# A batch loop written out in full on all five engines of a gated cross-attention kernel

## What is computed

```python
x = x + tanh(g_xattn[0]) * L0_xattn(layernorm(x), ctx)   # 4 heads of 64, q/k/v/o projections
x = x + tanh(g_ffn[0])   * L0_ffn(layernorm(x))          # x @ (W + low-rank product) + b
x = x + tanh(g_xattn[1]) * L1_xattn(layernorm(x), ctx)   # one head, softmax over 375 keys
x = x + tanh(g_ffn[1])   * L1_ffn(layernorm(x))          # 16-head self-attention + top 2 of 8 experts
```

## Time and profile before

| what | value |
|---|---|
| runs shown | 920.01, 922.46, 924.37 us; median 922.46 |
| profiled execution: its own time | 923.47 us |
| profiled execution: span, first to last instruction | 921.5 us |
| mean granted TensorE clock | 0.977 |
| busy over the span: PE, DVE, ACT, POOL | 846.2 (92%), 785.2 (85%), 563.2 (61%), 392.7 (43%) us |
| instructions recorded | 34388 |
| DMA packets: the kernel's own (q1), instruction fetch (q8, q14) | 41256; 18 and 11 |

### The profile page before, as it was taken

How to read it: one execution, slowest core, us unless ns; L and a number is a source line. 1 busy time by engine, 2 the same in 40 slices (tenths; PEclk the granted TensorE clock), 3 DMA queues, 4 the chain that set the end, 5 groups by cost and what they waited for, 6 DMA issues and landing times. The chain is left out here.

```text
span 921.5 us, 34388 instructions
## 1 busy us (share of the span) xinstructions
PE 846.2 (92%) x11764; PEld 666.0 (72%) x11764; DVE 785.2 (85%) x1910; ACT 563.2 (61%) x1230; POOL 392.7 (43%) x603
## 2 busy tenths in 40 slices
PE   4678999999999999999999999999999999999876
PEld 2467777778777777787777778777777787777654
DVE  3588989989998989899899998998999889888654
ACT  2444666666666666666666666666666666666443
POOL 3311545433455453344554433445544334454433
PEclk9789999999999999999999999999999999999987
DMA  7311222121112211212222122122221211111100
GB/s 257 114 61 57 66 79 66 59 73 61 58 61 75 75 62 62 68 57 63 64 75 74 52 73 63 53 70 66 75 70 54 75 60 56 61 59 56 39 6 6
DMA packets 41285, 61.82 MB, mean 67 GB/s; under 512 B 6158, under 2 KB 28036, under 8 KB 41128
## 3 DMA queue, kind: packets, MB, share of 16 engines
q1 hardware_dynamic: 41256, 61.43, 20.9%
HBM read 37.77 MB, written 3.67 MB: 45 GB/s over the span
## 5 line engine op out<-in xcount | busy, mean ns | idle before, releaser
L1317 POOL TENSOR_TENSOR acc<-part,acc 112x256 f32<-112x256 f32 x256 | 212.4, 830 | 298.9 <-DVE acc L1163 275.3
L820 ACT ACTIVATE part<-bankE,cgS 112x256 f32<-112x256 f32 x256 | 107.2, 473 | 3.0 <-PE bankE L329 2.3
L1266 POOL TENSOR_SCALAR ln_ve<-ln_mv 112x1 f32<-112x1 f32 x128 | 33.9, 265 | 174.5 <-DVE ln_mv L967 173.2
L329 PE MATMUL bankE<-wexs_hi,xT_hi 128*112 128x512 f16 x256 | 99.3, 388 | 3.4 <-ACT part L820 3.4
L1270 POOL TENSOR_TENSOR ln_rs<-ln_ve,cst 112x1 f32<-112x1 f32 x128 | 94.5, 738 | 10.7
L329 PE MATMUL bankE<-wexs_hi,xT_lo 128*112 128x512 f16 x256 | 97.7, 382 | 0.0
L329 PE MATMUL bankE<-wexs_lo,xT_hi 128*112 128x512 f16 x256 | 97.7, 382 | 0.0
L1067 DVE TENSOR_TENSOR p_lo<-p2T,p_hi 112x896 f16<-112x896 f32 x64 | 67.6, 1094 | 9.6 <-ACT p_hi L811 9.6
L1130 DVE TENSOR_REDUCE mx<-quad 112x8 f32<-112x896 f32 x64 | 69.6, 1088 | 1.0
L740 ACT ACTIVATE p0T<-quad 125x896 f32<-125x896 f32 x64 | 46.2, 722 | 38.6 <-PE quad L445 38.6
L973 DVE TENSOR_SCALAR xn<-x,ln_mv,ln_rs 112x256 f32<-112x256 f32 x96 | 54.9, 572 | 5.9 <-POOL ln_rs L1270 2.0
(11 more groups left out here) (239 smaller groups left out, 3275.5 us busy)
## 6 DMA issues: line engine op xcount, KB each, us to landing
ctf<-in_ctx_T SPq DMA_DIRECT2D x32, 375.0 KB, 3.1
ctn<-in_ctx_n SPq DMA_DIRECT2D x32, 375.0 KB
kvB<-kvA SPq DMA_DIRECT2D x32, 281.2 KB, 2.4
kc<-kvB SPq DMA_DIRECT2D x32, 187.5 KB
xin<-in_x SPq DMA_DIRECT2D x32, 112.0 KB, 2.0
x<-in_x SPq DMA_DIRECT2D x32, 112.0 KB, 2.1
out_x<-xout SPq DMA_DIRECT2D x32, 112.0 KB, 1.9
wex<-in_w_exp SPq DMA_DIRECT2D x1, 2048.0 KB, 9.9
```

Source lines behind the costliest of these rows:

```text
L329: last = mm(o, w, m, start=(n == 0), stop=(n == len(terms) - 1))
L820: act.activation(part[:, e, :], bankE[0:LQ, n * D:(n + 1) * D], ACT.Identity, scale=cgS[:, e:e + 1])\
L1317: pool.tensor_tensor(acc[:], part[:, 2 * j + n, :], acc[:], ALU.add).then_inc(moe_sum[j].sem, 1)
```

## The change

The hardware loops go. `iterations` and SP's loop become Python loops over all 36 iterations, so that each engine's program is one straight line, with every batch number an integer: counts in waits and addresses in DMAs become constants, the register steps that worked them out and the branch at the end of each iteration are gone. The order of steps in each iteration, the conditions of the waits and all operations on data are as they were.

```diff
-PEEL = 5
@@
         def iterations(eng, body):
-            for i in range(PEEL):
-                body(*at(i))
-            with eng.Fori(PEEL, NB) as i:
-                body(i, i - 1, i - 2, i - 3, i - 4)
-            for i in range(NB, NB + STAGES - 1):
+            for i in range(NB + STAGES - 1):
                 body(*at(i))
@@
-            for i in range(PEEL):
+            for i in range(NB - 1):
                 body(*at(i), True)
-            with sp.Fori(PEEL, NB - 1) as i:
-                body(i, i - 1, i - 2, i - 3, i - 4, True)
             for i in range(NB - 1, NB + STAGES - 1):
                 body(*at(i), False)
```

## The result

The changed kernel is slower: 950.93 us (median; 944.67 to 954.28) against 921.40 us (920.01 to 924.37) for the kernel before on the same chip, a ratio of 1.031 with a 95% interval of 1.025 to 1.037. The forecast of 935.5 had the sign and the place of the loss, but less than half its size, and the median lies 0.9 us above the range of 919 to 950.

The account below looks back on a forecast made before the run. A closed chain of two DMA copies and nearly full PE work, 26.45 us an iteration, was taken as the bound. 923.5 + 1.6 (steps, waits) + 11.5 (packets) = 936.6, less 1.0 offset: 935.5 us, range 919 to 950.

Parts of the forecast that it names:

- the sign and the place of the loss: Slower by 1.4%, through instruction packets delaying copies in the chain through SP; slower by over 0.5% had chance 0.70.
- The bound: Steady iterations: a closed chain from scores1_T through SP and two DMAs (10.97 us), then PE alone (15.48), sets the 26.45.
- Register steps, branches and waits, +1.6 us: Steady loop: PE part gains 0.14 us, DMA part loses 0.20; +0.06 an iteration over 27, bounds -3.8 to +5.4.
- Packets, count and rhythm: DMA queues in all 27 iterations: near 3 q8 and 2 q14 instruction packets each, drifting slowly, so hits come in phases.
- How often, and what one costs, 0.43 us an iteration: Copy landings: 0.53 q8 hits at 0.65 us plus 0.27 q14 hits at 0.3 an iteration; 11.5 us over 27.
- The clock: PE's wait before max0_T: one hit was not enough to lower PE's clock, so nothing was counted for it.
- the rival at 958 us: Fetch does more than touch landings: sequencers stop for code or two hits lower PE's clock; about 958 us, chance 0.08.
- Packets that miss: q8 packets stay off the copies or delays are absorbed; only small parts, -3.8 to +5.4, remain: about 924 us, chance 0.20.
- Branches on the path: PE's hand-over between iterations: removing 27 branches of 0.215 us saves 5.8 us, giving about 917 us; chance 0.10.

Follow-up runs that it names:

- the loop of three: The looped kernel before, with three iterations instead of one in its loop body on every engine: 983.55 us, ratio 1.064.
- the phase was locked at 1.0 to 1.5: Changed kernel plus 17 waits in each PE iteration from the sixth on and 96 instructions at PE's start: 995.71 us, ratio 1.077 to before.
- the locked clear phase: Changed kernel plus 17 waits in each PE iteration from the sixth on, keeping q8 packets off the copy: 932.64 us, ratio 1.009 to before.

## Why the prediction was right and wrong

*The bound.* Right. The chain of the earlier trace rows is what every loss with one buffer ran through, but for the loop of three; with it cut, PE's wait at `max0_T` was gone and the time fell by 27.6 us against before.

*Register steps, branches and waits, +1.6 us.* Right in size. PE's part is shorter by about 0.14 us a pass without clock falls (447.1 for 449.3 with one fall of 2.5 in it), SP's hops and the unhindered landing longer by 3.3 and 4.2 us over 29 passes, the hop behind it shorter by 1.5; together some +2. A clean pass of the changed kernel takes 26.49 to 26.51 us (the 16th, 18th and 20th) and one of before 26.44 to 26.49, some 0.04 us less, where the forecast had 0.06. The reading of the earlier trace rows was too coarse in one point: the 0.14 us are not PE's own. With PE alone straight its part stays at 15.47 us, and with PE looped and the rest straight it is 15.34.

*Packets, count and rhythm.* Right: near 3 on q8 and 2 on q14 an iteration, in phases. Passes 6 to 15 were hit, 16 to 20 nearly clean, 21 to 29 hit again, the 15 iterations worked out above.

*How often, and what one costs, 0.43 us an iteration.* This step failed first. It treated the packets as spread evenly over the iteration and priced each hit alike, 0.65 us. In the profiled run the 29 passes had 0.59 us of late landing each. A q8 packet started in the 3.5 us behind the issue in 18 of 29 passes, and in none in the 2.1 us before it (0.62, not 0.53), and the price hangs on where in them it starts:

| start of the q8 packet after the issue, us | passes | mean delay of the landing, us |
|---|---|---|
| 0 to 0.5 | 9 | 0.31 |
| 0.5 to 1.0 | 4 | 1.02 |
| 1.0 to 1.5 | 4 | 1.98 |
| later | 1 | 0.26 |

A mean over the 18 gives 0.83 us (in some a q14 packet lay there too). Where the phase was locked at 1.0 to 1.5, 16 passes had 2.05 us on average and 2.65 at most, above the 1.8 of the earlier trace rows that I had taken as the price of a square hit. The place is not the whole of it: one packet of that kernel started 2.10 us after the issue and went with a delay of 2.58. Against 11.5 us forecast, the late landings took 17.1 in 29 passes.

*The clock.* The second failed term, and the larger one for the median: "PE stood 1.96 us at full clock, so one hit is not enough". In the changed kernel the clock fell at 402, 566 and 812 us, each time behind a late landing (waits of 2.92, 1.60 and 2.76 us; one of 3.01 had no fall behind it), and PE's part took 16.47, 17.83 and 16.54 us instead of 15.3: 4.9 us. The other three timed runs had mean clocks about 0.011 below the profiled one; 0.011 of 943 is 10 us at most, and their median, 951.37, is 6.7 us longer. No trace of those runs shows where their clock fell, so that the remaining 6 us are clock is inferred from its mean. So of the two mis-sized terms the late landings took 5.6 us more than forecast, and the clock, put at nothing, 4.9 us in the profiled execution and, by that inference, about 11 in the median. This was the rival at 958 us, to which I gave 0.08; its clock part was real, its stops of sequencers were not, except in the loop of three.

*The rivals.* "Packets that miss" is the locked clear phase, 9 us above before, not 0: possible, but not what 17 instructions of drift give. "Branches on the path", 917, is wrong with one buffer, and with two the loops that cost were mostly those of other engines than PE, which the 215 ns of the earlier trace rows said nothing about.

## What to carry to other kernels

Before a loop is written out, ask what its body's instructions are fetched over. Here they came as packets on DMA queues beside the data, and a closed chain of short DMAs paid for those that fell on one of its copies; 96 instructions added at the start of the program shifted the price from 9 to 72 us. Cut the chain first (a second buffer was worth 27.6 us against before and made the packets harmless), and only then count branches. And measure a longer loop body before relying on it: here two iterations (about 1500 PE instructions) ran without fetches and three (about 2300) stopped PE at the head of each trip.

## What the runs showed of the hardware that I had not expected

- With a q8 packet beginning 1.0 to 1.5 us after the issue of `kvB<-kvA` it landed 2.0 us late on average and 2.65 at most; with one beginning at 0 to 0.5 us, 0.3. Why the place matters so much (other loads are issued right behind the copy) was not tried.
- After a wait of PE of 1.54 us (1.70 in the other kernel) its granted clock was halved for 6.8 us, at a cost of 2.5 us, in two kernels at the same pass. No pass with a shorter wait had a fall, and half of those with a longer one had none either.
- A looped body of three iterations was slower (983.55 us) than code with no loop at all (950.93).
- The loops of ACT, DVE and POOL cost PE three times what PE's own loop costs it, 0.23 against 0.07 us an iteration, in one profiled execution of each kernel.
